# One core, cross-attention and FFN block: the last eight units of attention regrouped in the hand-written order

## What is computed

```python
# cross-attention, 32 heads of 128, on layernorm(x)
xn  = rmsnorm(layernorm(x), ln_weight)
q, k, v = xn @ w_q.T, ctx @ w_k.T, ctx @ w_v.T          # each 1024 x 4096
score = einsum("bqhd,bkhd->bhqk", q, k) + position_bias
score = softmax(where(mask, score, -inf))                # rows without a valid key give 0
x = x + layernorm(x) + einsum("bhqk,bkhd->bqhd", score, v) @ w_out.T
# feed-forward, on layernorm(x)
r   = softmax(xf @ gate_w.T)                             # 8 experts
x = x + xf + ((xf * (r @ in_scale)) @ sign(weight).T) * (r @ out_scale) + bias
```

## Time and profile before

| | |
|---|---|
| median of three runs | 800.29 us (799.83 to 800.47) |
| the profiled execution | 800.21 us |
| its span, first to last instruction | 798.4 us |
| TensorE matmul busy | 793.6 us, 99% of the span |
| VectorE, ScalarE, GpSimd busy | 633.1, 352.9, 298.5 us |

### The profile page before, as it was taken

How to read it: one execution, slowest core, us unless ns; L and a number is a source line. 1 busy time by engine, 2 the same in 40 slices (tenths; PEclk the granted TensorE clock), 3 DMA queues, 4 the chain that set the end, 5 groups by cost and what they waited for, 6 DMA issues and landing times.

```text
span 798.4 us, 12698 instructions
## 1 busy us (share of the span) xinstructions
PE 793.6 (99%) x4090; PEld 675.5 (85%) x4090; DVE 633.1 (79%) x1066; ACT 352.9 (44%) x949; POOL 298.5 (37%) x279
## 2 busy tenths in 40 slices
PE   9999999999999999999999999999999999999998
PEld 7888888888888888888888888888888888888886
DVE  6877878886893596889988879788877978877775
ACT  6633432432341253554534345343534434446683
POOL 3123021020111032746455446554544654434136
PEclk9999999999999999999999999999999999999999
DMA  8464674575456648627566666656665675653002
GB/s 302 146 200 171 223 247 137 177 256 171 154 183 212 210 160 274 212 68 233 168 216 206 195 183 200 224 153 212 199 213 154 207 225 159 200 195 139 1 1 106
DMA packets 103217, 145.54 MB, mean 182 GB/s; under 512 B 9944, under 2 KB 74584, under 8 KB 97648
## 3 DMA queue, kind: packets, MB, share of 16 engines
q1 hardware_dynamic: 102720, 144.33, 55.7%
q10 hardware_dynamic: 432, 0.39, 0.2%
HBM read 93.31 MB, written 51.38 MB: 181 GB/s over the span
## 4 chain that ended last, share of the span: by engine, by line
PE 98%; DMA 1%; DVE 0%; issue 0%; ACT 0%; SPq 0%; DVEq 0%
PE out L1470 11%; PE out L1472 11%; PE out L1471 11%; PE proj L1470 11%; PE proj L1472 11%; PE proj L1471 10%; PE s L1564 7%; PE o L1591 4%; PE s L1471 4%; PE s L1472 4%; PE s L1470 4%; PE t L1591 3%; PE proj L1667 1%; PE proj L1668 1%; PE t L1619 1%; PE t L1575 1%
## 5 line engine op out<-in xcount | busy, mean ns | idle before, releaser
L872 POOL TENSOR_TENSOR w_stage<-w_stage 128x256 f32<-128x256 f32 x30 | 26.9, 898 | 262.9 <-DMA w_stage<-in_wk 241.4
L896 POOL TENSOR_TENSOR bias_mask<-bias_raw,mask_neg 128x512 f32<-128x512 f32 x64 | 75.3, 1184 | 81.4 <-DVE s L1306 67.4
L1042 ACT ACTIVATE s<-s,neg_max 128x128 f32<-128x128 f32 x208 | 71.5, 349 | 52.5 <-DVE neg_max L1309 52.5
L1470 PE MATMUL out<-wo_hi,o_hi 128*128 128x512 f32 x224 | 88.5, 395 | 0.0
L1472 PE MATMUL out<-wo_lo,o_hi 128*128 128x512 f32 x224 | 87.8, 392 | 0.0
L1471 PE MATMUL out<-wo_hi,o_lo 128*128 128x512 f32 x224 | 87.3, 390 | 0.0
L1470 PE MATMUL proj<-x_hi,w_hi 128*128 128x512 f32 x210 | 85.0, 405 | 0.0
L884 POOL TENSOR_TENSOR w_lo<-w_stage,w_hi 128x512 fp32r<-128x512 f32 (+1 forms) x52 | 59.4, 1155 | 68.1 <-ACT w_hi L988 68.1
L1472 PE MATMUL proj<-x_lo,w_hi 128*128 128x512 f32 x210 | 82.5, 393 | 0.0
L1471 PE MATMUL proj<-x_hi,w_lo 128*128 128x512 f32 x210 | 82.0, 390 | 0.0
L1347 DVE TENSOR_TENSOR acc<-out,acc 128x512 f32<-128x512 f32 x100 | 67.2, 673 | 14.1 <-PE out L1472 14.0
(11 more groups left out here) (370 smaller groups left out, 2123.5 us busy)
## 6 DMA issues: line engine op xcount, KB each, us to landing
k_spill<-ring SPq DMA_DIRECT2D x64, 256.0 KB, 3.4
v_spill<-ring SPq DMA_DIRECT2D x64, 256.0 KB, 2.5
p_turned<-probs SPq DMA_DIRECT2D x208, 64.0 KB, 2.8
probs_t<-p_turned SPq DMA_DIRECT2D x52, 256.0 KB, 2.9
big_stage<-in_wv SPq DMA_DIRECT2D x8, 1024.0 KB, 8.7
w_stage<-in_wq SPq DMA_DIRECT2D x32, 256.0 KB, 3.5
k_first<-k_spill SPq DMA_DIRECT2D x8, 1024.0 KB, 7.3
v_first<-v_spill SPq DMA_DIRECT2D x8, 1024.0 KB, 9.7
```

The costliest lines, as they stand in the source:

```text
L896: pool.tensor_tensor(bias_mask[:, j % 2], bias_raw[:, i % 2][:, None, :].to_broadcast([P, HALF, P]), mask_neg[:, halves[half], :], ALU.add ...
L1042: last = act.activation(scores_of(j)[:, b], scores_of(j)[:, b], ACT.Exp, bias=neg_max[:, col:col + 1], accum_out=row_sum[:, col:col + 1])
L1470: pe.matmul(to[:], left_hi, right_hi, start=first and n == 0, stop=False, skip_group_check=True)
```

## The change

It is in `schedule` and in one line of `context_bank`. No instruction is added or removed: the list has the same 2360 steps in another order, except that unit 55's context sum goes to bank o instead of bank t.

```diff
@@ biased: no bias load past the last (unchanged in effect) @@
-        if bias_of(j + 2) != bias_of(j + 3):
+        if bias_of(j + 2) < len(BIASES) - 2 and bias_of(j + 2) != bias_of(j + 3):
@@ units 54 and 55, and the last keys' load @@
-        steps += aside(j + 2, outs(o, 5) + prod[2], [*outs(o, 6), *sums[:1]], outs(o, 7) + [("WO", p)])
+        steps += aside(j + 2, [*outs(o, 5), *prod[2], ("KL", p + 2)], [*outs(o, 6), *sums[:1]], outs(o, 7) + [("WO", p)])
         if final:
-            steps += aside(j + 3, prod[5] + prod[7], [("WOL", p + 1), ("PV", j + 2), *prod[3], *prod[4], ("KL", p + 2), ("WO", p + 1)],
-                           [*outs(p, 0, 1), ("PV", j + 3), ("VV", p + 2)])
+            steps += aside(j + 3, prod[5] + prod[7], [("WOL", p + 1), ("PV", j + 2), ("S", j + 5), *prod[3], ("EXP", j + 5), *biased(j + 4),
+                                                      *prod[4], ("WO", p + 1)],
+                           [*outs(p, 0), ("N", j + 5), *outs(p, 1)])
@@ units 56 to 61: slot and swift are gone @@
-    steps += [("FW",)]
-    steps += [("SCALES",)]
-    steps += swift(j, outs(a, 2), [("SCALESL",), *outs(a, 3)], [("WOL", c), ("SIGN", 0)])
-    steps += swift(j + 1, outs(a, 4), outs(a, 5), [("SIGN", 1), ("WOH", c)])
-    steps += swift(j + 2, outs(a, 6), outs(a, 7), [("SIGN", 2)])
-    steps += swift(j + 3, outs(b, 0), [("WOLO", c), *outs(b, 1)], [("SIGN", 3)])
-    steps += [("S", j + 5), ("OUT", b, 2), ("T", j + 4), ("EXP", j + 5), ("BM", j + 6), ("OUT", b, 3)]
+    def together(j, late, *rest):
+        exps = [("EXP", j + 2)] if j + 3 < len(UNITS) else []
+        return [("PV", j - 1), ("T", j), ("S", j + 2), *late, *exps, *(biased(j + 1) if j + 3 < len(UNITS) else []), *rest]
+    steps += together(j, [("VV", c), ("FW",), ("SCALES",)], *outs(a, 2), ("SCALESL",), *outs(a, 3), ("N", j + 2), ("WOL", c))
+    steps += together(j + 1, [("SIGN", 0)], *outs(a, 4, 5), ("N", j + 3))
+    steps += together(j + 2, [("WOH", c)], *outs(a, 6, 7), ("N", j + 4))
+    steps += together(j + 3, [("SIGN", 1)], *outs(b, 0), ("WOLO", c), *outs(b, 1), ("N", j + 5))
+    steps += together(j + 4, [("SIGN", 2)], *outs(b, 2, 3), ("N", j + 6))
+    steps += together(j + 5, [("SIGN", 3)])
@@ the list by hand, up to where both are alike again @@
-    steps += [("PV", 60), ("S", 62), ("N", 61), ("OH", 60), ("S", 63), ("SC", 62), ("T", 61), ("OUT", 15, 1), ("OL", 60), ("EXP", 62),
-              ("BM", 63), ("SC", 63), ("OUT", 15, 0), ("PT", 61), ("ADD", 15, 1), ("EXP", 63), ("OUT", 15, 2), ("ADD", 15, 0), ("N", 62),
-              ("PV", 61), ("ST", 0), ("OUT", 15, 3), ("OH", 61), ("ADD", 15, 2), ("OL", 61), ("T", 62), ("ADD", 15, 3), ("OUT", 14, 4),
-              ("PT", 62), ("ST", 2), ("ST", 1), ("PV", 62), ("ST", 3), ("OUT", 14, 5), ("LN2", 0), ("ROOT", 0), ("OH", 62), ("LS", 0),
-              ("OUT", 14, 6), ("N", 63), ("NT", 1), ("NT", 0), ("OL", 62), ("T", 63), ("TX", 1), ("BI", 0), ("PT", 63), ("TX", 0), ("PV", 63),
+    steps += [("OUT", 15, 1), ("OUT", 15, 0), ("ADD", 15, 1), ("ADD", 15, 0), ("PV", 61), ("OH", 61), ("T", 62), ("PT", 62), ("EXP", 63), ("OL", 61),
+              ("OUT", 15, 2), ("ADD", 15, 2), ("OUT", 15, 3), ("N", 63), ("ST", 1), ("ST", 0), ("ADD", 15, 3), ("PV", 62), ("T", 63), ("OH", 62),
+              ("ST", 2), ("PT", 63), ("OUT", 14, 4), ("ST", 3), ("OUT", 14, 5), ("LN2", 0), ("ROOT", 0), ("OL", 62), ("LS", 0), ("OUT", 14, 6),
+              ("NT", 1), ("NT", 0), ("TX", 1), ("BI", 0), ("TX", 0), ("PV", 63),
@@ context_bank @@
-            return t_bank if j in BLOCKED and j % 2 else o_bank
+            return t_bank if j in BLOCKED and j % 2 and j != BLOCKED[-1] else o_bank
```

More of the change, by code:

```diff
@@ L265, in normal @@
         return [("N", j), ("TZ", j), ("TS", j)] if j in BLOCKED else [("N", j)]
-    def swift(j, early, middle, late):
-        return slot(j, early, middle, late, copy_first=True)
     def outs(p, *which):
@@ L328, in schedule @@
     a, b, c = SPLIT // 2 - 1, SPLIT // 2, SPLIT // 2 + 1
-    steps += [("FW",)]
-    steps += [("SCALES",)]
-    steps += swift(j, outs(a, 2), [("SCALESL",), *outs(a, 3)], [("WOL", c), ("SIGN", 0)])
-    steps += swift(j + 1, outs(a, 4), outs(a, 5), [("SIGN", 1), ("WOH", c)])
-    steps += swift(j + 2, outs(a, 6), outs(a, 7), [("SIGN", 2)])
-    steps += swift(j + 3, outs(b, 0), [("WOLO", c), *outs(b, 1)], [("SIGN", 3)])
-    steps += [("S", j + 5), ("OUT", b, 2), ("T", j + 4), ("EXP", j + 5), ("BM", j + 6), ("OUT", b, 3)]
-    steps = [part for step in steps for part in parts_of(step)]
-    steps += [("PV", 60), ("S", 62), ("N", 61), ("OH", 60), ("S", 63), ("SC", 62), ("T", 61), ("OUT", 15, 1), ("OL", 60), ("EXP", 62),
-              ("BM", 63), ("SC", 63), ("OUT", 15, 0), ("PT", 61), ("ADD", 15, 1), ("EXP", 63), ("OUT", 15, 2), ("ADD", 15, 0), ("N", 62),
[17 rows of a table removed]
-              ("SUM", 5), ("OS", 7), ("MP", 6), ("M", 7, 1), ("OSC", 7), ("SUM", 6), ("M", 7, 0), ("MPL", 1), ("SUML", 1), ("MPL", 0),
-              ("SUML", 0)]
+    def together(j, late, *rest):
[7 more added lines that the diff above has]
+    steps += together(j + 5, [("SIGN", 3)])
+    steps = [part for step in steps for part in parts_of(step)]
+    steps += [("OUT", 15, 1), ("OUT", 15, 0), ("ADD", 15, 1), ("ADD", 15, 0), ("PV", 61), ("OH", 61), ("T", 62), ("PT", 62), ("EXP", 63), ("OL", 61),
[16 rows of a table added]
+              ("SUM", 4), ("M", 6, 1), ("SUM", 5), ("OS", 7), ("MP", 6), ("M", 7, 1), ("OSC", 7), ("SUM", 6), ("M", 7, 0), ("MPL", 1), ("SUML", 1),
+              ("MPL", 0), ("SUML", 0)]
     return steps
```

## The result

| | kernel before | changed kernel |
|---|---|---|
| median of 15 runs each, same call | 800.07 us | 801.81 us |
| ratio | | 1.0021, 95% interval 1.0014 to 1.0028 |
| the profiled execution shown here | 800.21 us | 801.32 us |
| its span | 798.4 us | 799.4 us |

The kernel is slower by 1.74 us. The forecast was 0.7 us slower, with a range of 799.7 to 802.0 us. So the sign and the range hold, and the size does not: more than half of the loss is missing from the forecast's sum.

What follows compares the result with a forecast made beforehand. The prediction took TensorE, 99% busy, to bound the kernel. TensorE gains 0.27 us on the way, yet the end chain makes TX 0 0.69 us later, carried whole: +0.7 on 800.21 gives 800.9 us, range 799.7 to 802.0.

Steps and rivals of the forecast that it cites:

- What bounds the kernel: Whole span: TensorE is 99% busy with no other engine on the path, so reordering gains only where TensorE waits.
- The loss at the end: End of attention: EXP 63, N 63 and OL 62 delay the normalised tiles, so TX 0 starts 0.69 us later.
- only TensorE counts: Rival, 25%: the chain at the end is shorter, TX 1 starts when asked, 799.9 us.
- the regrouping does nothing: Rival, 3%: 0.03 us per block is rounding and the chain fits in the slack; 800.2 us.
- The load of the keys: KL 15 ahead of TL 54: TL 54 lands at 708.2, PV 54 asks at 709.20, so no wait.
- The chance of 10% that PV 54 would wait: Rival, 10%: at 709.20 the key load makes TL 54 land late; 801.8 us, at the far end 804.1.
- The gain on TensorE: PV 54 to TX 1: fewer separate 128-column blocks and no PV 57 wait make TensorE alone 0.27 us faster.
- the wait of PV 57: PV 57 waits for PT 57 behind SIGN 0; with PT 57 ahead, 0.09 us goes.
- 6 x 0.03: PV 54 to TX 1: 9 returns to 512-column work instead of 15, at 0.03 us each, save 0.18 us.
- What lies beside it at no cost: Units 56 to 62: looser chains SC, EXP, N, and S 57 moved up six microseconds, cost nothing.
- The clock: Rival, 1%: the clock falls to 1.2 GHz for one unit's 5 us in the PV, T, S block; 805 us.
- The chances: Whole kernel: 88% for same within 0.2% (1.6 us), 9% for slower by more, 3% for faster by more.

Runs made afterwards that it cites:

- e1: The changed kernel run again without an edit: 801.88 us, ratio 1.0021 to the kernel before.
- e2: Changed kernel with EXP 63 and N 63 ahead again and OL 62 behind LS: 800.77 us, ratio 1.0004.
- e10: Changed kernel with only EXP 63 and N 63 early, OL 62 left between LN2 and LS: 800.82 us, ratio 1.0006.
- e6: Changed kernel with EXP 63 and N 63 early, OL 62 behind LS, and ADD 13 1 ahead of N 57: 799.99 us, ratio 0.9999.
- e8: Changed kernel with EXP 63, N 63 early, OL 62 behind LS, ADD 13 1 ahead of N 57, KL 15 behind unit 55's stores: 800.27 us, ratio 1.0004.
- e12: The kernel before run once more for a second profile, without an edit: 800.55 us.
- e5: Changed kernel with ADD 13 1 ahead of N 57 on VectorE: 801.16 us, ratio 1.0013.
- e7: Changed kernel in its own order, with GpSimd's WOLO 14 computing only 8 of 1024 columns: 800.87 us, ratio 1.0007.
- e3: Changed kernel with key load KL 15 behind unit 54's load and unit 55's stores: 801.77 us, ratio 1.0017.
- e9: Changed kernel with only OL 62 moved behind LS: 801.55 us, ratio 1.0014.
- e11: The changed kernel run once more for a second profile, without an edit: 801.82 us.
- e4: Kernel before with only key load KL 15 moved up ahead of TL 54: 800.24 us, ratio 0.9997.

## Why the prediction was right, and where it was not

**What bounds the kernel:** right. TensorE's list is the path; each shift in it arrived at the end of the kernel within 0.15 us.

**The loss at the end:** right in mechanism, place and size. PV 54 came 0.36 us later in e1 than in the earlier trace rows, so 0.36 is to be added to the forecast's times. T 62: 747.55 against 747.62 measured. N 63: 750.35 against 750.46. LN2: 754.52 against 754.58. LS: 755.64 against 755.67. NT 1: 756.05 against 756.06. The waits before TX 1 and TX 0 were put at 0.6 and 0.35; measured are 0.61 and 0.27 (TX 1 to TX 0 takes 0.71, not 0.44). That the first agrees to 0.01 is partly luck: by the forecast TX 1 is asked for at 756.21 and starts at 756.81, and both came 0.11 or 0.12 us later. e2 and e10 show by removal that it is this chain and that EXP 63 with N 63 carries it. The rival that only TensorE counts falls with that, and so does the one that the regrouping does nothing.

**The load of the keys:** right, with less cover than it seemed. TL 54 landed at about 708.1 in e2 against 708.2 foreseen, and at about 709.4 in e1, 0.8 us later when e1's 0.36 is taken off, still in time. In e6 it was not in time, by the 0.25 us above. The rule cited from the Trainium skill, "DMA: Bandwidth & Descriptors", section on queues, rings and completion order, is that each engine takes the descriptors of a row in ring order; 8.3 us with the keys ahead against 4.6 without agree with it. That no small load can pass is the forecast's own step: the same section adds that completion is not in order of issue. The chance of 10% that PV 54 would wait was fair: one profile of nine has it, and e1 had 0.2 us to spare.

**The gain on TensorE:** right in sign, too large. Of the two profiles without a hole, e8 asks for TX 1 at 755.88 - 709.15 = 46.73 us behind PV 54, and e6 at 755.80 - 708.99 = 46.81, with the 0.11 us of PV 54's late row in it, against 756.12 - 709.20 = 46.92 before. The gain is 0.1 to 0.2 us, not 0.27, and 0.09 of it is the wait of PV 57. So at most 0.10 is left of the 0.18 for the regrouping itself. The term that was mis-sized is "6 x 0.03": that a return to 512-column work costs 0.03 us was one difference of two rounded starts. Unit for unit, PV 56 to PV 57 takes 4.96 us in e1 and 5.00 before, PV 57 to PV 58 4.95 and 5.09, PV 58 to PV 59 5.01 and 5.02, PV 59 to PV 60 5.02 and 5.01: beside PV 57's 0.09 that is 0.04 and 0.05 us in two units and nothing in the other two. Against e12's profile the stretch would gain 49.14 - 48.62 = 0.52 us, most of it PV 57's wait, which the forecast took from one execution where it was short.

**What lies beside it at no cost:** this is the step that failed. It said that the chains of units 56 to 62 become looser and that S 57 goes up at no cost. It followed S 57 and SC 57, and for SC 57 the reads behind it on VectorE. It did not follow N 57, which goes up with them: from 721.76 us to 716, where WOLO 14 runs on GpSimd, and ahead of ADD 13 1, whose bank TensorE wants at once. In the trace of the kernel before it could be read when WOLO 14 runs, and what a GpSimd instruction does to N 57. N 57's small product there, and on GpSimd WOLO 14 (L905) and the BM beside N 57 (L896):

```profile
721.76 0.80 DVE L1315 TENSOR_TENSOR inv_sum<-inv_sum,row_valid 128x4 f32<-128x4 f32 x1
...
715.25 2.37 POOL L905 TENSOR_TENSOR w_lo<-wo_raw,w_hi 128x1024 fp32r<-128x1024 f32 x1 [5.69 <-ACT w_hi L1068]
...
721.38 1.16 POOL L896 TENSOR_TENSOR bias_mask<-bias_raw,mask_neg 128x512 f32<-128x512 f32 x1 [0.17 <-POOL x_lo L926]
```

0.80 us instead of 0.16 for 128 x 4 elements, ending with GpSimd's instruction. Whoever had asked why would have looked for what runs on GpSimd at the new place. e5 and e7 show this term from two sides.

With it the sum is 0.88 for the end (0.61 and 0.27), 0.93 for the hole before OUT 13 3 (the mean of 50.46 and 50.47, less e5's 49.54), less 0.11 (e5 asks for TX 1 46.81 us behind PV 54): 1.70 us, and 50.46 - 48.77 is 1.69. The medians say 1.74. Their parts agree with the rows roughly: against the kernel before of its own group e1 is 1.60 us slower, e2 0.49, e5 1.08 and e7 0.79, and e6 is 0.09 faster, so e2 takes back 1.1, e5 0.5, e7 0.8 and e6 all of it. Where one of these is off its 0.9, the difference is within the intervals, which are some 0.7 us to either side. That most of the changed kernel's runs have the second hole is an inference: five of the six profiled kernels with that order have it (e2, e3, e9, e10, e11), one does not (e1).

**The clock:** no part in it. Every slice is in the highest tenth.

**The chances:** 88% stood on a change within 0.2%. The ratio is 1.0021 with an interval from 1.0014 to 1.0028, so it lies on that line, a little beyond it. The forecast gave what lies beyond 9%, mostly for the key load, and that was the wrong mishap. That 801.81 us lies within the range is luck as well: the range reached up to 802.0 for a key load that lands late, and what filled the upper part of it was N 57's wait, which the forecast did not have.

## What to carry to other kernels

When a step goes up in a list that all engines walk, everything that it consists of goes up with it: for each of its instructions ask what runs beside it on the other engines at the new time, and which buffer is freed by what now stands behind it. Give that question first to small VectorE instructions with both inputs in SBUF near long GpSimd ones, and let whatever frees a bank for TensorE go ahead of them. Where the saving is a few hundredths of a microsecond per block, read it from whole units in several executions, not from one difference of starts; and where a list is full on TensorE, regrouping it has little to give and waits to lose, as here: with both repaired it is worth nothing that the medians show.

## What the runs showed of the hardware

**VectorE and GpSimd hold each other up for whole instructions.** A product of 128 x 4 elements took 0.16 us alone, and 0.80, 1.02 or 2.37 beside a GpSimd instruction, by how much was left of that when it started. A start 0.04 us ahead of GpSimd's let it through at 0.16 (e1). It goes the other way too: BM 59 took 1.62 us in e1, where the large product was running when it started, and 1.17 in e11. ADD (L1333) reads one input from PSUM and kept to 0.68 or 0.69 us, in e5 beside the running WOLO 14.

The Trainium skill, "SBUF — State Buffer", section "Who interferes with whom", states this: VectorE instructions with two inputs in SBUF contend with GpSimd instructions that read SBUF, at a port pair that both share and that is locked for a whole instruction, and the order of issue decides who waits. The traces agree: 2.37 us beside GpSimd's 2.36, and 0.19 when that instruction was cut to 0.20.

**Executions of one kernel differ by small stalls at places far from any edit.** The first profile of the kernel before and e12 differ by 0.4 us in one wait of PV 57, and e4's by 1.3 us between 285 and 337 us. There e4's trace lists two waits of TensorE for VectorE, 0.5 us each (L1160 and L1172); why they came in this execution stays open. For a change of this size one profiled execution gives the mechanism, and not the size.
